# Five layer norms between stages: scales by group of four tiles through logarithm and exponential, three of four low parts on GpSimd

## What is computed

```python
def _layernorm(x, axis=-1, eps=1e-05):
    m = jnp.mean(x, axis=axis, keepdims=True)
    v = jnp.var(x, axis=axis, keepdims=True)
    return (x - m) / jnp.sqrt(v + eps)

x = _layernorm(x + _L0_attn_ref(x, ...), axis=-1)
x = _layernorm(x + _L0_ffn_ref(x, ...), axis=-1)
x = _layernorm(x + _L1_attn_ref(x, ...), axis=-1)
x = _layernorm(x + _L1_ffn_ref(x, ...), axis=-1)
x = _layernorm(x + _L2_attn_ref(x, ...), axis=-1)
x = _layernorm(x + _L2_ffn_ref(x, ...), axis=-1)
x = _layernorm(x + _L3_attn_ref(x, ...), axis=-1)
x = _layernorm(x + _L3_ffn_ref(x, ...), axis=-1)
```

## Time and profile before

| | us |
|---|---|
| time, median of 3 runs | 2009.62 |
| the three runs | 2012.48, 2007.04, 2009.62 |
| the profiled execution | 2013.46 |
| its span in the profile | 2011.7 |
| busy in it: TensorE, DVE, ScalarE, GpSimd | 1736.3, 1581.1, 1251.7, 360.0 |

### The profile page before, as it was taken

One profiled execution on the slowest core, in us unless ns is written; L12 is line 12 of the kernel. 1 busy time (PEld: TensorE's weight loads), 2 busy tenths in 40 slices (PEclk: granted clock), 3 DMA queues, 4 the chain that ended last, 5 costly groups with the idle time before them and its releaser, 6 DMA issues. The chain is left out here.

```text
span 2011.7 us, 46155 instructions
## 1 busy us (share of the span) xinstructions
PE 1736.3 (86%) x16491; PEld 1088.0 (54%) x16498; DVE 1581.1 (79%) x3789; ACT 1251.7 (62%) x3209; POOL 360.0 (18%) x476
## 2 busy tenths in 40 slices
PE   5999978866859999948769999999969999998685
PEld 4999953444534444426544444444436666665453
DVE  4444458988878999987879999999967887777663
ACT  5666637743425655556438888888856666665565
POOL 1000001200011111110001122212214343445111
PEclk7555568978869999979879999999979999999797
DMA  3200006300004444300026666666610000000000
GB/s 79 63 4 4 4 12 252 115 13 1 0 15 178 159 163 161 132 1 1 0 79 246 234 225 222 233 231 222 227 66 22 22 3 21 22 1 1 2 2 22
DMA packets 51669, 174.04 MB, mean 87 GB/s; under 512 B 7104, under 2 KB 32448, under 8 KB 34112
## 3 DMA queue, kind: packets, MB, share of 16 engines
q1 hardware_dynamic: 50368, 170.09, 23.4%
q10 hardware_dynamic: 1152, 1.90, 0.3%
HBM read 167.45 MB, written 2.95 MB: 85 GB/s over the span
## 5 line engine op out<-in xcount | busy, mean ns | idle before, releaser
L865 DVE TENSOR_TENSOR ps<-ps,m_comb 128x512 f32<-128x512 f32 x520 | 363.4, 699 | 23.9 <-DMA m_comb<-m_shares 7.2
L850 DVE TENSOR_TENSOR m_hwlo<-ps,m_hwhi 128x512 f16<-128x512 f32 x520 | 354.0, 681 | 0.3
L826 ACT ACTIVATE m_hwhi<-ps 128x512 f16<-128x512 f32 x520 | 308.2, 593 | 20.9 <-DVE ps L865 19.4
L832 ACT ACTIVATE ps<-ps 128x512 f32<-128x512 f32 x388 | 225.9, 582 | 81.7 <-PE ps L782 81.5
L782 PE MATMUL ps<-x_hi,m_whi 128*128 128x512 f16 x652 | 250.2, 384 | 8.5 <-DVE m_hwlo L850 4.6
L782 PE MATMUL ps<-x_lo,m_whi 128*128 128x512 f16 x652 | 250.1, 384 | 0.0
L782 PE MATMUL ps<-x_hi,m_wlo 128*128 128x512 f16 x652 | 249.8, 383 | 0.0
L755 POOL CAST m_whi<-m_stage 128x256 f16<-128x256 f32 (+1 forms) x130 | 55.2, 424 | 903.4 <-PE ps L788 633.0
L464 DVE TENSOR_TENSOR rn_s_lo<-rn_s_full,rn_s_hi 128x32 f16<-128x32 f32 x512 | 98.7, 193 | 133.0 <-ACT rn_s_full L421 133.0
L788 PE MATMUL ps<-m_hwhi,m_whi 128*128 128x512 f16 x520 | 197.7, 380 | 0.4 <-DVE m_hwlo L850 0.2
L788 PE MATMUL ps<-m_hwlo,m_whi 128*128 128x512 f16 x520 | 197.6, 380 | 0.0
(11 more groups left out here) (449 smaller groups left out, 4006.0 us busy)
## 6 DMA issues: line engine op xcount, KB each, us to landing
m_comb<-m_shares SPq DMA_DIRECT2D x128, 1024.0 KB, 5.1
m_stage<-in_m_w SPq DMA_DIRECT2D x97, 128.0 KB, 4.5
m_stage<-in_m_w SPq DMA_DIRECT2D x33, 192.0 KB, 4.6
kept_lj_w<-in_lj_w SPq DMA_DIRECT2D x6, 1024.0 KB, 5.0
kept_lq_w<-in_lq_w SPq DMA_DIRECT2D x1, 1600.0 KB, 7.8
kept_la_w<-in_la_w SPq DMA_DIRECT2D x1, 1280.0 KB, 5.4
rn_rows<-in_L_attn_rows SPq DMA_DIRECT2D x4, 256.0 KB, 4.3
rn_xs<-rn_xn_hi SPq DMA_DIRECT2D x32, 32.0 KB, 1.9
```

The source lines that it names most:

```text
L826: nc.scalar.activation(hw_hi[:, k % HB, :], weighted(k), ACT.Copy).then_inc(hi_done, 1)
L832: nc.scalar.activation(acted(k), ps[:, 4, :] if gated else bank(k), func).then_inc(act_done, 1)
L850: nc.vector.tensor_tensor(hw_lo[:, k % HB, :], weighted(k), hw_hi[:, k % HB, :], ALU.subtract)\
L865: nc.vector.tensor_tensor(weighted(k), bank(k), comb[:, s, n * QW:(n + 1) * QW], ALU.mult)\
```

## The change

The five norms after stages 0 to 4 get a function of their own, `norm_phase`; the last one keeps `layernorm_phase`. In the new function:

- statistics, aggregation and scale go by group of four tiles instead of by half of eight;
- the scale is Exp(-0.5 x Ln(variance + eps)), both on ScalarE, in place of Sqrt on ScalarE and reciprocal on DVE; the table set is preloaded at the head of ScalarE's part;
- ScalarE normalises groups 0, 1 and the first two tiles of group 3; DVE group 2 and the last two tiles of group 3, after ScalarE is done with its two (they share a bank);
- ScalarE's copies to `xT` come after all its normalising; DVE makes all four `x_hi`, the last `x_lo` too; GpSimd makes the `x_lo` of groups 0 to 2, each after its `x_hi`, and waits for its last one.

```diff
+def norm_phase(nc, S):
+    ps, ident, src, dst = S.psum, S.ident, S.rT, S.xT
+    NORMED_ACT, NORMED_DVE = (1, 2, 2, 3), (0, 0, 1, 2)
...
+            def turn_back(g):
+                pe.wait_ge(normed_act, NORMED_ACT[g])
+                if NORMED_DVE[g]:
+                    pe.wait_ge(normed_dve, NORMED_DVE[g])
+                for j in range(4):
+                    last = nc.tensor.transpose(ps[:, G + g, j * P:(j + 1) * P], rows[:, 4 * g + j, :], ident[:])
+                last.then_inc(back, 1)
...
+        @block.vector
+        def _(dve):
+            def statistics(g):
+                dve.wait_ge(rows_in, g + 1)
+                for i in range(4 * g, 4 * g + 4):
+                    last = nc.vector.bn_stats(stats[:, i, :], ps[:, g, i % 4 * C:(i % 4 + 1) * C])
+                last.then_inc(stats_s, 1)
+                dve.wait_ge(stats_s, g + 1)
+                for i in range(4 * g, 4 * g + 4):
+                    last = nc.vector.bn_aggr(mv[:, i, :], stats[:, i, :])
+                last.then_inc(aggr_s, 1)
...
+            def high(g):
+                dve.wait_ge(copied, g + 1)
+                nc.vector.tensor_copy(S.x_hi[:, cut(g)], dst[:, cut(g)]).then_inc(high_s, 1)
+
+            statistics(0)
+            statistics(1)
+            shift(0)
+            statistics(2)
+            shift(1)
+            statistics(3)
+            normalise(2, range(4))
+            shift(3)
+            dve.wait_ge(normed_act, 3)
+            normalise(3, range(2, 4))
+            for g in range(G):
+                high(g)
+            dve.wait_ge(high_s, G)
+            nc.vector.tensor_tensor(S.x_lo[:, cut(G - 1)], dst[:, cut(G - 1)], S.x_hi[:, cut(G - 1)], ALU.subtract)
+
+        @block.scalar
+        def _(act):
+            nc.scalar.preload_act_table_set("natural_log_exp_and_others")
+
+            def scale(g):
+                act.wait_ge(aggr_s, g + 1)
+                nc.scalar.activation(logv[:, tiles(g)], mv[:, tiles(g), 1], ACT.Ln, bias=S.eps_ap(LN_EPS)).then_inc(log_s, 1)
+                act.wait_ge(log_s, g + 1)
+                nc.scalar.activation(rstd[:, tiles(g)], logv[:, tiles(g)], ACT.Exp, scale=-0.5).then_inc(rstd_s, 1)
...
+            scale(0)
+            scale(1)
+            normalise(0, 1, range(4))
+            scale(2)
+            normalise(1, 2, range(4))
+            scale(3)
+            normalise(3, 3, range(2))
+            for g in range(G):
+                copy(g)
+
+        @block.gpsimd
+        def _(pool):
+            for g in range(G - 1):
+                pool.wait_ge(high_s, g + 1)
+                nc.gpsimd.tensor_tensor(S.x_lo[:, cut(g)], dst[:, cut(g)], S.x_hi[:, cut(g)], ALU.subtract).then_inc(low_s, 1)
+            pool.wait_ge(low_s, G - 1)
...
-            if k not in "56":
-                layernorm_phase(nc, S, rT, xT, out=out if k == STAGES[-1] else None)
+            if k in "01234":
+                norm_phase(nc, S)
+            if k == STAGES[-1]:
+                layernorm_phase(nc, S, rT, xT, out=out)
```

More of the change, by code:

```diff
@@ L181, in _, with tiles, cut, turn_in @@
                 sp.wait_ge(stored, 16 * G)
+def norm_phase(nc, S):
+    rows_in, stats_s, aggr_s, log_s, rstd_s, shift_s, normed_act, normed_dve, back, copied, high_s, low_s = S.sems.new(
+        *(f"nm_{n}" for n in ("rows_in", "stats", "aggr", "log", "rstd", "shift", "normed_act", "normed_dve", "back",
+                              "copied", "high", "low")))
+    G = NT // 4
+    ps, ident, src, dst = S.psum, S.ident, S.rT, S.xT
+    NORMED_ACT, NORMED_DVE = (1, 2, 2, 3), (0, 0, 1, 2)
+    with (nc.sbuf_tensor(f"nm_stat{S.sems.n}", [P, NT, 6], F32) as stats,
+          nc.sbuf_tensor(f"nm_mv{S.sems.n}", [P, NT, 2], F32) as mv,
+          nc.sbuf_tensor(f"nm_lg{S.sems.n}", [P, NT], F32) as logv,
+          nc.sbuf_tensor(f"nm_rs{S.sems.n}", [P, NT], F32) as rstd,
+          nc.sbuf_tensor(f"nm_sh{S.sems.n}", [P, NT], F32) as shifts,
+          nc.sbuf_tensor(f"nm_x{S.sems.n}", [P, NT, C], F32) as rows,
+          nc.Block(no_gpsimd_drain=True) as block):
+        def tiles(g):
+            return slice(4 * g, 4 * g + 4)
+        def cut(g):
+            return slice(g * QW, (g + 1) * QW)
+        @block.tensor
+        def _(pe):
+            def turn_in(g):
+                for j in range(4):
+                    i = 4 * g + j
+                    last = nc.tensor.transpose(ps[:, g, j * C:(j + 1) * C], src[:, i * P:(i + 1) * P], ident[:])
+                last.then_inc(rows_in, 1)
+            def turn_back(g):
+                pe.wait_ge(normed_act, NORMED_ACT[g])
+                if NORMED_DVE[g]:
+                    pe.wait_ge(normed_dve, NORMED_DVE[g])
+                for j in range(4):
+                    last = nc.tensor.transpose(ps[:, G + g, j * P:(j + 1) * P], rows[:, 4 * g + j, :], ident[:])
+                last.then_inc(back, 1)
+            for g in range(G):
+                turn_in(g)
+            for g in range(G):
+                turn_back(g)
+        @block.vector
[9 more added lines that the diff above has]
+                last.then_inc(aggr_s, 1)
+            def shift(g):
+                dve.wait_ge(rstd_s, g + 1)
+                nc.vector.scalar_tensor_tensor(out=shifts[:, tiles(g)], in0=mv[:, tiles(g), 0], scalar=-1.0,
+                                               in1=rstd[:, tiles(g)], op0=ALU.mult, op1=ALU.mult).then_inc(shift_s, 1)
+            def normalise(g, some):
+                dve.wait_ge(rstd_s, g + 1)
+                for i in some:
+                    last = nc.vector.tensor_scalar(rows[:, 4 * g + i, :], ps[:, g, i * C:(i + 1) * C], mv[:, 4 * g + i, 0:1],
+                                                   rstd[:, 4 * g + i:4 * g + i + 1], ALU.subtract, ALU.mult)
+                last.then_inc(normed_dve, 1)
+            def high(g):
[11 more added lines that the diff above has]
+            normalise(3, range(2, 4))
+            for g in range(G):
+                high(g)
[9 more added lines that the diff above has]
+                nc.scalar.activation(rstd[:, tiles(g)], logv[:, tiles(g)], ACT.Exp, scale=-0.5).then_inc(rstd_s, 1)
+            def normalise(g, count, some):
+                act.wait_ge(shift_s, count)
+                for i in some:
+                    n = 4 * g + i
+                    last = nc.scalar.activation(rows[:, n, :], ps[:, g, i * C:(i + 1) * C], ACT.Identity,
+                                                bias=shifts[:, n:n + 1], scale=rstd[:, n:n + 1])
+                last.then_inc(normed_act, 1)
+            def copy(g):
+                act.wait_ge(back, g + 1)
+                nc.scalar.activation(dst[:, cut(g)], ps[:, G + g, :], ACT.Copy).then_inc(copied, 1)
+            scale(0)
[5 more added lines that the diff above has]
+            normalise(3, 3, range(2))
+            for g in range(G):
+                copy(g)
[5 more added lines that the diff above has]
+            pool.wait_ge(low_s, G - 1)
```

## The result

Over nine runs of each the changed kernel took a median of 2014.89 us (2014.22 to 2017.08) against 2011.78 (2003.65 to 2013.31) for the kernel before. The ratio of the means is 1.0026, with a 95% interval of 1.0014 to 1.0039, that is +5.2 us with an interval of +2.8 to +7.8 (the medians alone differ by 3.1). It is slower, by somewhat less than the 0.3% that was set as the bound, so it falls in the case that was given 0.38. The forecast was +7.0, and the time lies inside the range of 2010 to 2021. That range also holds the 2011.78 of the kernel before, and the interval of the time holds +7.0. The windows of the norms, which repeat far more closely, are what tests the forecast.

What follows compares the result with a forecast made beforehand. Each norm stands between barriers, so its last-ending engine bounds it: 9.67 plus 4.88 us of shared lane gives 14.55 against 13.15, 1.4 us a norm, +7.0 over five. With 2009.6 that makes 2016.6 us, range 2010 to 2021.

Steps and rivals of the forecast that it cites:

- the case that was given 0.38: Whole kernel: time the same, within 0.3% (6.0 us) of the kernel before; chance 0.38.
- The front half: Norm up to the last normalisation: scales per group of four, DVE's last two tiles done at 9.32 us, first cast 9.25 to 9.67.
- the three signs of being wrong: Casts keeping 0.42 us beside GpSimd, group-wise front ending before 9.3 us, or routers' first matmuls changing their granted clock.
- The earlier start buys nothing: Norm's turning back: first group starts 1.5 us sooner, at 5.3, but the last still ends at 10.46 us.
- the table loads are hidden: Start of each norm: ScalarE's preload (old load 1.28 us) lies under the statistics, since aggregation 0 ends at 2.0 us.
- The step that carried the sign: Norm's back half: casts and subtractions of DVE and GpSimd share one lane, 4.88 us from 9.67, ending at 14.55.
- The held-back remainders: Back half: what a held DVE instruction still needs after release, about 0.28 us per cast and 0.55 for low(3).
- the lower bound of 14.1: Norm's end if GpSimd's start-up hides in its waiting: 14.1 us, +0.95 a norm, +4.8 in all.
- The order that I had left open: Back half: whether high(3) or low(1) goes first in the shared lane, said to change the order and not the sum.
- no blocking: First rival, back half: casts and GpSimd subtractions overlap, norm ends at 13.2, +0.3 us, 2010 us in all; chance 0.15.
- the clock: Second rival: earlier turning back keeps TensorE's clock high into next stages, some 11 us won, 2005.6 us; chance 0.08.
- the third rival: Back half: blocking at whole instruction length, norm ends at 15.3 us, +10.8 in all, 2020.4 us; chance 0.15.

Runs made afterwards that it cites:

- e1: Changed kernel with all four x_lo back on DVE and nothing on GpSimd; last x_lo at 12.91 us, time 1.0008 of the kernel before.
- e2: Changed kernel with DVE's casts and its one subtraction reading x from PSUM instead of SBUF; last x_lo at 13.23 us, five windows 71.31 us.
- e3: Kernel before with only the back half changed (GpSimd makes x_lo of groups 0 to 2); last x_lo at 14.16 us, five windows 75.69 us.
- e6: Changed kernel, DVE normalising all group 3, turning order 0, 2, 1, 3, GpSimd and ScalarE casting, DVE subtracting from PSUM; 0.9961 of the kernel before.
- e9: The kernel before, unchanged, profiled and timed again; five windows 70.68 us, time 1.0003 of the kernel before.
- e11: e6 timed again, unchanged; five windows 63.21 us, time 0.9974 of the kernel before.
- e12: Repeat of changed kernel with DVE normalising all group 3, order 0, 2, 1, 3, all casts and subtractions on DVE; 0.9990 of the kernel before.

## Why the prediction was right, and where it was off

The front half came as worked out, within 0.15 us. In the forecast's count, from the table load, the first turning back was due at 5.3 and came at 5.23, the last two normalisations at 9.32 and came at 9.21, the first cast at 9.25 and came at 9.12. One of the three signs of being wrong that the prediction named, a front that ends before 9.3, was therefore met, by 0.1 us; the other two were not. "The earlier start buys nothing" is nearly so: the whole new front is worth 0.2 us a norm (e1), through a second copy that is ready sooner. That the table loads are hidden holds: Ln started at 2.06. The load in the stage after the first norm did fall away and was worth nothing: the softmax's Exp came 9.88 us after that stage's first matmul, against 9.89 before.

The step that carried the sign, that casts and subtractions share one lane with GpSimd, is shown by e2 (e3 shows that the back half holds the whole loss, and e6 agrees). Its size was off: the term was 4.88 us from the end of the first cast, and it measured 4.48 (277.42 to 281.90). The held-back remainders were right (0.29 and 0.55 against 0.28 and 0.55). Two parts were too large. From the end of the first cast to the end of the first subtraction the sum had 0.28 + 1.16 = 1.44 us, and it took 1.35, as DVE issued the second cast right behind the first (277.34), before GpSimd had begun. And a GpSimd subtraction that is held behind a DVE cast has part of its own start done meanwhile: from the end of one to the end of the next were 1.29 us, where the sum took 1.44; this counts twice. With the front's 0.13 that is +0.87 us for the first norm instead of +1.4: its last `x_lo` ended at 14.02, just under the lower bound of 14.1 that the prediction worked out for its own mechanism. Four norms grew by 0.87 and the second by 0.6, 4.1 us in all, against +5.2 and +4.0 in the time. So the cause was right, and the size of the held lane, of which +7.0 was made, was too large by 0.4 us a norm.

The order that I had left open was a strict alternation from the third cast on: GpSimd, DVE, GpSimd, DVE.

The rivals: no blocking fell with the stretched casts. For the clock, windows of the changed kernel, the first norm's opening up to the first turning back and the router products, against the earlier trace rows:

```profile
267.92:273.10 5.18, 1.95 (x16) 1.71 (x16) 4.40 (x30) 3.69 (x10) 0.00 (x0) 1.00 0.01 3
282.89:290.10 7.21, 6.96 (x32) 6.86 (x32) 0.45 (x3) 1.47 (x8) 3.94 (x8) 0.50 0.25 75
```

The clock was still at the high level when the first turning back began, and the four turnings of that group took 0.66 us; the next eight, from 274.92, took 1.97, at the low level (0.50). The first group was turned at the high level in three of the five norms; in the second and fourth it too was at the low level, in 1.12 us. The router products after the norm took 6.96 us at the low level, exactly as before: the clock gave nothing back. Full lengths, the third rival, were too slow (15.3 for 14.02): of a held instruction 0.13 to 0.16 us was done by the handover.

The rule of the Trainium skill (SBUF — State Buffer, Who interferes with whom) was borne out in both kinds: casts, and the instruction with two SBUF inputs. What the Trainium skill calls blocking there was a little less than the whole instruction here, by those 0.13 to 0.16 us. The drain of 1.38 us after a table load of the Trainium skill (ScalarE: Activation LUTs, What ACT_TABLE_LOAD costs) would have put the first Ln at 2.7 us at the earliest; it started at 2.06, and ScalarE had been waiting for DVE's aggregation until then, so here the trace disagrees.

## What to carry to other kernels

Before moving half of an elementwise chain to GpSimd, look in the trace for DVE instructions that end just after a GpSimd one: here a float32 to float16 cast from SBUF to SBUF, and a subtraction with two SBUF sources, did not run beside a GpSimd subtraction. Give each engine reads that do not meet: DVE may take its operand from the PSUM bank, which was slower by itself (0.68 against 0.42 us for the cast) and faster in company (0.68 against 1.24 to 1.36). And in a chain between two barriers look for what normalises the last group; a first group that was ready 1.5 us sooner moved the end by 0.2.

## What the runs showed of the hardware

A granted clock of 1.00 in a view can mean that the profile holds no record of it. Windows of the opening 250 us, the kernel before in its first profile and in its second (e9):

```profile
0.00:250.00 250.00, 225.07 (x6341) 222.48 (x6342) 109.19 (x530) 153.72 (x1019) 6.57 (x8) 0.55 0.11 31
```

```profile
0.00:250.00 250.00, 226.17 (x6375) 223.58 (x6376) 109.67 (x533) 154.60 (x1023) 6.56 (x8) 1.00 0.11 31
```

This looks as if the second had run at the high level. But the first profile's records of the clock begin at 23 us, and the second's only at 264 us; where none stands, the view gives 1.00. The durations of TensorE's float16 matmuls of 128x128 tell the level. Where the first profile has a record of 1.00, all 804 took 217 to 230 ns. In the opening all 342 of the first profile, at 0.50, took 267 or 268 ns, and so did all 344 of the second. So both ran at the low level. The mean granted clock of the whole, 0.87 in the one and 0.94 in the other, differs for the most part by this gap; in e11 and e12 (0.93) the records likewise begin only at 267 us. Read a mean clock beside the duration of one form of matmul.

The windows of a norm repeat closely where the totals do not: those of the kernel before agree to 0.01 us each between two profiles whose totals differ by 7 us, and those of the changed kernel to 0.07. They move by up to 0.4 where the low clock falls in the opening, as in e6, and by 0.3 in the second norm with GpSimd's being at work. Where a change touches such closed windows, they settle its sign with one profile, while nine runs of each kernel left the total uncertain by some 2.5 us.
